# Two expert FFN blocks with attention between: selection, scatter, gather and row loads of the sorted experts placed anew

## The reference, cut to what matters

```python
x = Z                                     # 1024 tokens of 256 numbers
x = x + 0.5 * L0_ffn(layernorm(x))        # dense FFN + 8 experts, top 2
x = x + L0_attn(layernorm(x))             # relu attention, 4 sequences of 256
x = x + 0.5 * L0_ffn(layernorm(x))
x = x + 0.5 * L1_ffn(layernorm(x))        # 8 experts, all computed, top 4 weighted
x = x + L1_attn(layernorm(x))             # 16 heads, causal, ALiBi
x = x + 0.5 * L1_ffn(layernorm(x))
...
def L0_ffn(h):
    d = rms(gelu(rms(h) @ w_gate) * (rms(h) @ w_up) @ w_down)      # 256 -> 1024 -> 256
    top_w, top_i = top_k(softmax(router(rms(h))), 2)               # of 8 experts
    m = rms(sum over the two experts e of w_e * (gelu(h @ g_e) * (h @ u_e) @ d_e))
    return rms(d + m)
```

## Time and profile before

| what | value |
|---|---|
| median of 3 runs | 547.72 us (546.81 to 548.55) |
| profiled execution, its own time | 547.49 us |
| its span | 545.6 us |
| PE busy | 470.0 us, 86% |
| DVE, ACT, POOL busy | 366.2, 270.5, 158.8 us |
| mean granted TensorE clock | 0.961 of 2.4 GHz |
| HBM | 26.47 MB read, 16.25 MB written |
| the three routed blocks, by the first transposes of each | 81.13, 164.07, 246.59, and 317.67 for the ffn1 block behind |

### The profile page before, as it was taken

The page is one execution under the profiler, slowest core; times in us unless marked ns, Lnnn a source line. Parts: engine busy times, 40 slices in busy tenths (PEclk is TensorE's granted clock), DMA queues, the critical chain, the costliest instruction groups (busy, mean ns, idle before and its releaser), DMA issues.

```text
span 545.6 us, 9564 instructions
## 1 busy us (share of the span) xinstructions
PE 470.0 (86%) x3062; PEld 403.4 (74%) x3062; DVE 366.2 (67%) x1181; ACT 270.5 (50%) x599; POOL 158.8 (29%) x224
## 2 busy tenths in 40 slices
PE   2999998957998777999878898489968999899996
PEld 1888886857887667887778776378856777668885
DVE  4569786638264768364758249779848878737876
ACT  3657632523445444454644455346455766644441
POOL 2001000331006241006330055336802333414442
PEclk9999999879999799999989998989999999999999
DMA  6332430031324222322133430058187540000011
GB/s 202 115 89 88 125 108 0 20 112 43 108 89 153 68 87 59 107 79 86 40 106 108 115 100 19 12 113 123 35 266 238 154 118 2 2 2 0 2 40 38
DMA packets 35327, 45.96 MB, mean 84 GB/s; under 512 B 4400, under 2 KB 27824, under 8 KB 35280
## 3 DMA queue, kind: packets, MB, share of 16 engines
q1 hardware_dynamic: 31920, 38.55, 24.5%
q0 software_dynamic: 2304, 6.29, 3.6%
q10 hardware_dynamic: 1056, 0.52, 0.3%
HBM read 26.47 MB, written 16.25 MB: 78 GB/s over the span
## 4 chain that ended last, share of the span: by engine, by line
PE 55%; DVE 16%; POOL 7%; issue 7%; DMA 6%; ACT 6%; SPq 2%; DVEq 0%; ACTq 0%; POOLq 0%
PE ps L756 13%; PE ps L758 13%; PE ps L757 13%; POOL z_rows L689 4%; DMA stage<-z_rows 3%; DVE x L2092 3%; PE ps L942 2%; PE ps L1216 2%; PE ps L1168 2%; DVE bn L1676 2%; DMA z_rows<-z,slots_u 1%; PE ps L1289 1%; PE ps L1199 1%; DVE ps L2175 1%; PE ps L771 1%
## 5 line engine op out<-in xcount | busy, mean ns | idle before, releaser
L756 PE MATMUL ps<-zh,w0u_h 128*128 128x512 f32 x160 | 66.3, 414 | 1.5 <-DVE zl L1703 1.5
L757 PE MATMUL ps<-zh,w0u_l 128*128 128x512 f32 x160 | 64.8, 405 | 0.0
L758 PE MATMUL ps<-zl,w0u_h 128*128 128x512 f32 x160 | 64.6, 404 | 0.0
L756 PE MATMUL ps<-w0d_h,ah 128*128 128x256 f32 (+1 forms) x205 | 60.2, 294 | 2.0 <-DVE al L1810 1.6
L2092 DVE SCALAR_TENSOR_TENSOR x<-ps,aff,x 128x256 f32<-128x256 f32 x128 | 52.9, 475 | 9.6 <-PE ps L758 8.1
L758 PE MATMUL ps<-w0d_l,ah 128*128 128x256 f32 (+1 forms) x205 | 58.8, 287 | 0.0
L757 PE MATMUL ps<-w0d_h,al 128*128 128x256 f32 (+1 forms) x205 | 58.7, 287 | 0.0
L656 POOL TENSOR_TENSOR al<-act,ah 128x512 fp32r<-128x512 f32 x32 | 41.6, 1301 | 49.8 <-ACT ah L1503 46.6
L756 PE MATMUL ps<-w_h,ah 128*128 128x256 f32 x128 | 37.6, 293 | 12.7 <-DVE x L2092 10.0
L2175 DVE CUSTOM_DVE_ANT_0 ps<-ps,bias 128x256 f32<-128x256 f32 (+1 forms) x128 | 42.5, 384 | 7.9 <-PE ps L1168 7.1
L1798 DVE TENSOR_TENSOR act<-gel,ps 128x512 f32<-128x512 f32 x40 | 27.3, 684 | 25.8 <-ACT gel L1356 25.8
(11 more groups left out here) (231 smaller groups left out, 1350.3 us busy)
## 6 DMA issues: line engine op xcount, KB each, us to landing
stage<-in_w_dram SPq DMA_DIRECT2D x16, 384.0 KB, 3.1
stage<-z_rows SPq DMA_DIRECT2D x21, 256.0 KB, 2.8
y_rows<-tmp SPq DMA_DIRECT2D x21, 256.0 KB, 2.2
qs<-split_out SPq DMA_DIRECT2D x24, 128.0 KB, 2.6
ks<-split_out SPq DMA_DIRECT2D x48, 64.0 KB, 2.5
stage<-in_w_dram SPq DMA_DIRECT2D x8, 256.0 KB, 2.8
z_rows<-tmp SPq DMA_DIRECT2D x1, 1920.0 KB, 8.2
ks<-pad SPq DMA_DIRECT2D x6, 256.0 KB, 9.6
```

The lines of the kernel that those rows point to most:

```text
L756: pe.matmul(o, lh, rh, start=start, stop=False, **kw)
L757: pe.matmul(o, ll, rh, start=False, stop=False, **kw)
L758: return pe.matmul(o, lh, rl, start=False, stop=stop, **kw)
```

## The change

All edits concern the routed blocks and the first ffn1 block:

- **Selection.** PE turns the logits back, and counts the ranks, between the two halves (gate and up) of unit 0 and unit 1. DVE selects in unit 0 ahead of its product, makes the places in unit 1 ahead of `act_lo`, and does `left_acc` and `dense_norm` behind the product of unit 1.
- **Scatters.** They are called tile by tile. In block 1 the root of the experts' part (`moe_rms`) moves from ahead of all eight scatters to between the fourth and fifth.
- **Gathers.** Both rows of a tile are fetched one after the other, with a semaphore for each tile; `dense_rms` comes ahead of the last tile. Scaling and summing move a unit earlier, and wait tile by tile. In the ffn1 block they are spread over units 1 and 2, the squares go from unit 3 to 2, the sum's squares from 4 to 3, `moe_norm` from 4 to 3, `finish0` and the next layernorm's statistics from 5 to 4.
- **Raw rows.** `stage` is seen as three places of two tiles (`Z_RING`), each with its semaphore; SP loads three units ahead.
- **Later weights.** Three sets in units 2 to 4 of block 2, three in units 2 to 4 of block 3, two in units 14 and 15 of block 3. SP issues the loads of these two together, behind the store of pair unit 11 of the block.
- **Hosted attention** starts at unit 9, not 8; the layernorm ahead of it comes in units 7 and 8 (was 6 and 7), the one behind it in units 13 and 14 (was 12 and 13). In block 3 the layernorm's two parts come in units 8 and 10 (was 7 and 9).

```diff
-W1_BLOCK = 2
+Z_RING = 3
...
         def later_weights(fb, v):
-            if fb == W1_BLOCK:
-                return {0: (0, 1), 1: (2,), 2: (3,), 3: (4,), 4: (5,)}.get(v, ())
-            return (dense_unit(v),) if fb == f0 - 1 and v >= LAST else ()
+            if fb >= f0 - 2 and 2 <= v < 5:
+                return v - 2 + 3 * (fb - f0 + 2)
+            return dense_unit(v) if fb == f0 - 1 and v >= LAST else None
...
-        FIN = 6
+        FIN, HOST = 6, 9
...
-                return 5 if b == 0 else 4
+                return 5 if b == 0 and st.before != "ffn0" else 4
...
             def load_rows(n):
-                v = n % U0
-                if v >= DENSE + 2:
-                    sp.wait_ge(ztp_ps, pair_no(n) - 1)
-                sp.dma_start(z_slot(n), slot_rows(z_rows, n)).then_inc(zrow_s[n % 2], 16)
+                q = pair_no(n)
+                if n % U0 >= DENSE + Z_RING:
+                    sp.wait_ge(ztp_ps, q - Z_RING + 1)
+                sp.dma_start(z_slot(n), slot_rows(z_rows, n)).then_inc(zrow_s[q % Z_RING], 16)
...
-                load_rows(first)
-                load_rows(first + 1)
+                for i in range(Z_RING):
+                    load_rows(U0 * fb + DENSE + i)
                 for v in range(DENSE, LAST + 2):
-                    if v + 2 < LAST and v >= DENSE:
-                        load_rows(U0 * fb + v + 2)
+                    if v + Z_RING < LAST:
+                        load_rows(U0 * fb + v + Z_RING)
                     if v >= DENSE + 2:
                         store_rows(U0 * fb + v - 2)
-                    if v >= LAST - 2 and v < LAST and fb == f0 - 1:
-                        sp.wait_ge(ztp_ps, PAIRS0 * (fb - 1) + v + 1 - DENSE)
-                        load_weights(U0 + v + DENSE + 2 - LAST)
+                    if v == LAST - 1 and fb == f0 - 1:
+                        sp.wait_ge(ztp_ps, PAIRS0 * fb)
+                        load_weights(U0 + DENSE)
+                        load_weights(U0 + DENSE + 1)
...
+            def gather_all(fb):
+                for t in range(BT):
+                    if t == BT - 1:
+                        dense_rms(fb)
+                    gather(fb, t)
...
-                            if fb == 1:
-                                moe_rms(0)
-                            else:
-                                gather(fb - 1)
-                                dense_rms(fb - 1)
-                            scatter(fb)
+                            if fb > 1:
+                                gather_all(fb - 1)
+                            for t in range(BT):
+                                if fb == 1 and t == BT - 2:
+                                    moe_rms(0)
+                                scatter(fb, t)
...
                         ups(n, 0)
+                        if v == 0:
+                            pe.wait_ge(acc_s, E - 1)
+                            if fb > 1:
+                                pe.wait_ge(x_s[hosted(fb - 1)], 2)
+                            logits(6, routed["ffn0", fb])
+                        if v == 1:
+                            ranks(fb)
...
-                    if v == 3 and fb > 1:
-                        scale_first(fb - 1)
+                    if v == 2 and fb > 1:
+                        for t in range(BT):
+                            scale_first(fb - 1, t)
...
+            def combine(fb, t):
+                dve.wait_ge(gath_s[t], 16 * TOP0 * fb)
+                dve.wait_ge(scaled_s, BT * (fb - 1) + t + 1)
...
+                        if v == 1:
+                            places(fb)
                         act_lo(n - 1)
-                    if v == 1:
+                    if v == 0:
                         take_logits(routed["ffn0", fb], 6)
                         shift_logits(routed["ffn0", fb], 2)
                         select(fb)
-                        left_acc(st, b, 1)
-                        if fb > 1:
-                            dense_norm(fb - 1)
-                    if v == 2:
-                        places(fb)
...
                     product(n)
+                    if v == 1:
+                        left_acc(st, b, 1)
+                        if fb > 1:
+                            dense_norm(fb - 1)
...
-                        if v == FIN:
+                        if v == FIN + 1:
                             prepare(2 * fb, 0)
-                        if v == FIN + 1:
+                        if v == FIN + 2:
                             prepare(2 * fb, 1)
                             attn0_xz(a)
```

117 lines of the change are left out of this document (54 added, 63 removed).

## The result

The changed kernel takes **522.28 us** (median of 4 runs, 522.06 to 523.03) against 547.26 for the kernel before in the same session (545.93 to 548.55): ratio 0.9546, 95% interval 0.952 to 0.9572. The forecast was 526 within 519 to 535. The profiled span fell from 545.6 to 520.0 us.

The account below looks back on a forecast made before the run. The chain from logits through selection and scatters to row loads was taken to bound units 0 to 5 of routed blocks, PE most of the rest. Blocks -8.1, -7.8, -5.0 and ffn1 -1.0 sum to -21.9: 526 us, range 519 to 535.

Parts of the forecast that it names:

- Selection and first `down0`: Routed blocks, units 0 to 2: earlier selection and places start PE's first `down0` sooner; -0.8, -3.7 and 0 us.
- a likely second drop of the clock: Block 2, first `down0`: PE's clock falls again behind the new wait, taking 0.8 of the 4.5 us gained.
- Scatters and rows: Routed blocks: earlier scatters remove PE's wait for the first raw rows; -6.0, -3.0 and -2.9 us, cover 1 to 3.
- The clock behind the waits: Routed blocks, behind the first row wait: matmuls no longer run at the slow clock; -1.2, -1.0 and -0.8 us.
- Ring: Block 3: loads behind the third place run one unit earlier, removing the later row waits; -3.3 us.
- Hosts one unit later: Blocks 1 and 2: shorter low-part wait -1.2 us each; layernorm delaying the next block's first turning +1.1 each.
- Last weights: End of block 3: the last two weight sets load 2.1 us later, so PE waits behind ACT; +2.0 us.
- L1 expert block: First ffn1 block: earlier `finish0` and statistics, but a 5 us PE wait with slow matmuls behind it; -1.0 us.
- more is won: First rival (10%): clock never drops behind new short waits, ffn1 gives its 2.4 us, block ends cost nothing; 518 us.
- Waits are traded: Rival (20%): middle units run into DVE and ACT, block 3's and the hosts' waits stay, clock drops; 534 us.
- POOL's DMAs hold up the selection: Rival (8%): blocks 2 and 3, gathers stall DVE's small steps, first `down0` 4 us later in both; 536 us.
- The serial loads: Rival (2%): row loads issue only when their unit is due, 3.0 us for each of 21 pair units; 589 us.

Follow-up runs that it names:

- late table: Changed kernel with the four DVE steps that make the table of experts by tile moved behind unit 1's product: 522.43 us, ratio 0.9551.
- early selection: Kernel before with only selection, ranks and places a unit earlier; weights, scatters, gathers, two row places and hosts as before: 537.53 us, ratio 0.9818.
- three moves: Changed kernel with gates in unit 11, first of the last two weight sets loaded ahead of a store, and `finish0` one position later: 515.58 us, ratio 0.9436.
- hosts as before: Changed kernel with hosted attention and layernorm work back at their old units, block 3's layernorm too: 527.71 us, ratio 0.9646.
- gates in unit 11: Changed kernel with a routed block's expert weights and gates computed in unit 11 instead of unit 14: 522.70 us, ratio 0.9567.
- two places: Changed kernel with two places for raw rows instead of three, all else kept: 525.92 us, ratio 0.9624.
- ring alone: Kernel before with three places for raw rows, plus the last weight sets' loads as the ring needs them: 543.03 us, ratio 0.9941.
- load early: Changed kernel with the first of the last two weight sets loaded by SP ahead of a store of rows: 521.07 us, ratio 0.9529.

## Why the prediction was right, and where it was off

**By its steps.** The first turning of raw rows splits each block in two. The measured differences, with my terms in brackets:

| stretch | block 1 | block 2 | block 3 |
|---|---|---|---|
| to the first turning of raw rows | -7.83 (-6.8) | -8.34 (-6.7) | -3.80 (-2.9) |
| from there to the block's end | -2.57 (-1.3) | -1.56 (-1.1) | -2.02 (-2.1) |

- *Selection and first `down0`.* Confirmed. The forecast wait for the four operations was about 1.7 us; it is 1.60, 1.49 and 1.50. The first `down0` (PE's first product with the dense down weights) of block 1 starts 1.45 us earlier in its block (the earlier trace rows less its start: 18.11, now 16.66); 1.5 was worked out. In block 2 it is 5.22 earlier, where I had 4.5. What I took off both for "a likely second drop of the clock" (0.7 and 0.8) was wrong: it never fell behind these waits.
- *Scatters and rows.* Confirmed, all three waits gone, and the root between the fourth and fifth scatter decides block 1 (+6.60 undone). That I took the early value was right: the fifth scatter started at 100.88, 0.9 us before my earliest. The cover was thinner than the 1 us I had put as its least: about 0.5 us in block 1, the estimate made with the late table.
- *The clock behind the waits.* This is the term that was mis-sized. I put 1.2, 1.0 and 0.8 us, for one slow stretch behind the row wait. Busy time shows 3.05, 3.35 and 1.72, 8.1 against 3.0. Blocks 1 and 2 of the kernel before had slow stretches behind the selection's wait as well (the 0.41 us matmul of the earlier trace rows was their sign), and I had let their end count as zero or as a loss.
- *Ring.* 3.65 us undone, 3.3 forecast, by the two waits named.
- *Hosts one unit later.* Forecast -1.2 +1.1, so nothing. The price was right (1.25 and 1.22 us for `z`); the gain was too small: undone, the blocks lost 2.3 to 2.8 us net. I had 1.8 us going and 0.6 coming back, and no clock.
- *Last weights.* ACT stands 3.70 us (forecast 3.4) and PE 2.30 (2.0); undone -2.46. The one part of the change that costs.
- *L1 expert block.* Forecast -1.0, measured +0.1. `finish0` starts 29.07 us into the block, not 31.14, so 2.07 earlier (2.5 forecast). But PE waits 1.84 us for `comb` at 308.93, which it didn't before, and its long wait is 5.89 us, where I had 5. With three groups of matmuls at the slow clock behind it, as forecast, nothing is left.

**By the total.** The three blocks gave 26.1 us, not 20.9. The L1 expert block withheld 1.1, and the unchanged rest and the start moved by +1.4 and -1.0, which no step of mine names; both are differences of PE's clock in code that is the same. So 526 became 522.3: the mechanism stands, the clock's share was too small, and the miss lies on the side of the first rival.

**The rivals.** Of the three causes of "more is won" one held: the clock stayed up. (Its price was 518.8 rather than 518, since the sum already held 1.0 of ffn1's 2.4.) The block ends did cost 1.2 us each, and ffn1 gave nothing. "Waits are traded" fell: it wanted the hosts' 1.2 us and the ring's 3.3 to stay. That POOL's DMAs hold up the selection fell too. In the changed kernel a gather runs on POOL from 162.03 to 163.09, and DVE's steps beside it are:

```profile
162.09 0.22 DVE L1744 TENSOR_REDUCE selm<-eq 128x32 f32<-128x64 f32 x1
162.34 0.18 DVE L1842 CAST sel_b<-selm 128x32 bf16<-128x32 f32 x1
...
163.73 0.22 DVE L1855 TENSOR_TENSOR r_lt<-lower,r_nt 128x64 bf16<-128x64 bf16 x1
```

The third line, a step with two inputs in SBUF, stands beside the next gather (163.40 to 164.35). All three take the same time in block 1, where POOL stands idle meanwhile (0.22, 0.18 and 0.22 us at 89.84, 90.10 and 91.45). By the rule cited for this rival (the Trainium skill, SBUF — State Buffer, on the ports) the one of DVE and GpSimd that starts second stands until the other is done, if DVE's operation runs in a mode with two ports or, against a GpSimd operation that reads SBUF, has two inputs in SBUF. For indirect DMAs beside these steps the trace does not show it. The serial loads did not come: PE waits for no load of rows.

## What to carry to other kernels

Price a wait of PE together with the slow matmuls behind it, and read both from one row of windows: length less busy is the wait, the change in busy time of the same matmuls is the clock. Here that was 18.0 and 8.1 us. Before moving a chain earlier, look for the one slow input that its queue serves first: four scatters ahead of a root that waits for another engine were worth 6.6 us in block 1, and the early selection without it 0.9 there. And do not discard a small gain that vanishes in the total before it was tried together with the removal of the next wait: three moves gave nothing clear of the noise by themselves and 6.0 us together.

## What the hardware showed that I had not expected

**The length of a wait does not tell whether the clock falls.** Behind 2.50 us at 121.94 (hosts as before) it was 0.50 some 2 us later. Behind 2.85 us at 131.73 in the kernel before it stayed up (and fell behind the same wait, 2.85 us at 128.25, in the kernel before with the early selection). The windows of 2 us around that wait:

```profile
129.00:131.00 2.00, 0.00 (x0) 0.00 (x0) 1.93 (x10) 0.30 (x1) 0.00 (x0) 1.00 0.19 66
131.00:133.00 2.00, 1.27 (x10) 1.11 (x11) 1.82 (x6) 0.61 (x2) 1.21 (x2) 1.00 0.00 0
133.00:135.00 2.00, 2.00 (x20) 2.00 (x19) 1.97 (x5) 0.72 (x3) 0.00 (x0) 1.00 0.00 0
```

And the wait for the last weights was followed by the slow clock in three kernels (2.26 us with the hosts as before and with the gates in unit 11, 2.40 with the table late) and not in the changed one (2.30) or with two places (2.83). What decides it beyond the wait was not settled. It makes every small gain uncertain by one slow stretch: that stretch cost 1.4 us of busy time in block 1 (hosts as before) and 1.8 in block 3 (gates in unit 11).

**Code that isn't touched changes its time with the clock.** The rest behind the L1 expert block took from 184.77 us (PE busy 165.76) to 188.49 (169.38) in profiles of kernels that have it word for word alike; the difference in busy time, 3.62 us, is nearly the whole difference in length. (The longest begins at the slow clock, left over from the L1 expert block.) The 1.4 us that the changed kernel lost there are of this kind: 2.09 more busy, 0.7 less idle. They are not plain scatter from profile to profile, though: the changed kernel and five of its variants took 187.12 to 187.39 us, the kernel before and the one with the early selection 185.90 and 186.15 (with the ring alone it was 188.33). Why the clock falls once more in some kernels was not found.

**Small DVE operations beside POOL's.** In the L1 expert block of the changed kernel one on 32 columns, 0.19 us elsewhere, took 2.88 us:

```profile
302.38 2.88 DVE L1749 TENSOR_TENSOR em<-lex,selm 128x32 f32<-128x32 f32 x1
```

POOL's three subtractions stand beside it:

```profile
302.68 3.82 POOL L660 TENSOR_TENSOR al<-act,ah 128x512 fp32r<-128x512 f32 x3
```

By the profile it begins 0.3 us ahead of them, against what I had argued from the earlier trace rows, and lasts until 305.26, when two of the three are done. An indirect DMA of POOL ran until 302.65, but that is not what held it: with the load early, the same operation lies wholly beside that DMA (300.95, the DMA from 300.86 to 301.81) and takes 0.19 us. Before, three other operations were caught, for 0.90, 1.21 and 1.27 us: which one it is depends on where POOL's work falls.
